# Token groups split on chip, 16-bit turns, joint gates and a folded right side in a fused transformer layer

## What is computed

```python
h = einsum('bhid,oi,od->bho', x, weighted_sum, weight)   # x: 4 x 512 x 256 x 4
h = concatenate([h, txt], axis=1)                        # 589 rows a batch
n = layernorm(h)
gate = sigmoid(relu(n @ gate_w1 + b1) @ gate_w2 + b2)    # 64, then 32 wide
S = cumsum(n @ V_w, axis=1)                              # over the rows
y = (gate * (n @ U_w) * S) @ out_w + out_b
h = h + conv3(n, conv_w) + y                             # three taps along the rows
m = layernorm(h)
q, s = round(m / s), max|m| / 127 per row                # the same for rhs, per column
h = h + (q @ q_rhs) * s * s_rhs
```

## Time and profile before

| | |
|---|---|
| Median of three timed runs | 111.67 us (110.92 to 111.87) |
| Profiled execution | 110.85 us, its span 109.0 us |
| TensorE busy | 98.9 us (91%) |
| VectorE busy | 82.7 us (76%) |
| ScalarE busy | 71.2 us (65%) |
| GpSimd busy | 63.7 us (58%) |
| Moved by transfers | 17.30 MB, 159 GB/s on average |

### The profile page before, as it was taken

How to read it: one execution, slowest core, us unless ns; L and a number is a source line. 1 busy time by engine, 2 the same in 40 slices (tenths; PEclk the granted TensorE clock), 3 DMA queues, 4 the chain that set the end, 5 groups by cost and what they waited for, 6 DMA issues and landing times.

```text
span 109.0 us, 2062 instructions
## 1 busy us (share of the span) xinstructions
PE 98.9 (91%) x660; PEld 85.3 (78%) x660; DVE 82.7 (76%) x239; ACT 71.2 (65%) x144; POOL 63.7 (58%) x111
## 2 busy tenths in 40 slices
PE   5999999999999999999999899997999879788630
PEld 5888888868878899799889799776996669676510
DVE  1456359653387678899897979989799799997991
...
GB/s 61 332 332 362 112 325 51 253 314 206 162 177 302 271 182 111 260 245 165 238 232 177 206 96 179 93 48 150 29 0 99 0 96 35 96 3 0 96 125 125
DMA packets 7993, 17.30 MB, mean 159 GB/s; under 512 B 839, under 2 KB 4783, under 8 KB 7855
## 3 DMA queue, kind: packets, MB, share of 16 engines
q0 software_dynamic: 2880, 10.49, 42.8%
...
q10 hardware_dynamic: 432, 0.27, 0.9%
...
## 4 chain that ended last, share of the span: by engine, by line
PE 65%; DVE 14%; ACT 7%; DMA 5%; issue 5%; POOL 2%; DVEq 0%; ACTq 0%
PE h_ps L796 20%; PE h_ps L808 7%; PE h_ps L810 6%; PE h_ps L812 6%; DMA x_low<-x_dram 5%; PE uvg_ps L873 5%; DVE tmp L752 4%; PE uvg_ps L880 4%; PE xt_ps L857 3%; PE acc_ps L938 2%; DVE nstep L726 2%; PE acc_ps L945 2%; ACT glob L541 2%; DVE amax L724 2%; DVE lscale L746 2%
## 5 line engine op out<-in xcount | busy, mean ns | idle before, releaser
L808 PE MATMUL h_ps<-w_high,x_high 128*128 128x256 f32 x80 | 24.2, 303 | 0.5 <-DMA x_low<-x_dram 0.5
L796 PE MATMUL h_ps<-w_tok,x_sb 128*128 128x256 f32 x96 | 22.5, 389 | 0.0
L810 PE MATMUL h_ps<-w_low,x_high 128*128 128x256 f32 x80 | 22.4, 279 | 0.0
L812 PE MATMUL h_ps<-w_high,x_low 128*128 128x256 f32 x80 | 22.3, 279 | 0.0
L796 PEld LDWEIGHTS h_ps<-w_tok,x_sb 128*128 128x128 f32 x96 | 18.4, 196 | 3.0 <-issue 0.4
L808 PEld LDWEIGHTS h_ps<-w_high,x_high 128*128 128x128 f32 x80 | 15.0, 188 | 3.0 <-issue 2.1
L369 POOL TENSOR_SCALAR rstd<-mv 128x2 f32<-128x2 f32 (+2 forms) x21 | 6.8, 322 | 17.0 <-DVE mv L623 16.6
L370 POOL TENSOR_TENSOR rstd<-rstd,exponent 128x2 f32<-128x2 f32 (+2 forms) x21 | 14.9, 712 | 1.7
L620 DVE BATCH_NORM_STATS2 stats<-h_ps 128x6 f32<-128x256 f32 (+1 forms) x36 | 13.6, 416 | 3.0 <-PE h_ps L796 2.8
L810 PEld LDWEIGHTS h_ps<-w_low,x_high 128*128 128x128 f32 x80 | 15.1, 188 | 0.1
L812 PEld LDWEIGHTS h_ps<-w_high,x_low 128*128 128x128 f32 x80 | 15.0, 188 | 0.0
...
## 6 DMA issues: line engine op xcount, KB each, us to landing
...
```

What stands on the lines that cost most here:

```text
L796: last = nc.tensor.matmul(h_of(g)[:, t, :], x_sb[:, g % 2, kc, t * P:(t + 1) * P], w_tok[:, kc, :], start=(kc == 0 and t == 0), stop=(kc = ...
L808: nc.tensor.matmul(h_of(g)[:, t, :], x_high[:, g % RING, kc, at], w_high[:, kc, :], start=(kc == 0 and t == 0), stop=False, skip_group_che ...
L810: nc.tensor.matmul(h_of(g)[:, t, :], x_high[:, g % RING, kc, at], w_low[:, kc, :], start=False, stop=False, skip_group_check=True)
L812: last = nc.tensor.matmul(h_of(g)[:, t, :], x_low[:, g % RING, kc, at], w_high[:, kc, :], start=False, stop=(kc == KC - 1), skip_group_che ...
```

## The change

It has these parts.
- *Split on chip.* Only group 0 stays plain (`PLAIN` = 1). For groups 1 to 3 (`BY_DMA` = 4) x comes by SyncE's plain loads into three slots; ScalarE rounds it (`chip_high`), and VectorE (groups 1 and 2, `chip_low`) or GpSimd (group 3, `pool_low`) subtracts, in two halves each. Group 3 needs none of the rounding and adding transfers any more.
- *16-bit turns.* The rounded values get another constant, so that the lower 16 bits of each hold the whole number, and `q_turn` transposes those 16 bits alone.
- *Gates.* Both halves' hidden rows lie in one tile of 128 rows, w2 stands twice on a diagonal of 128 x 128, and one product, one sigmoid and one GpSimd product of 64 rows serve a batch. Gate rows now land in the bank of the turns.
- *Text rows* are copied into the bank by ScalarE (`put_txt`).
- *Folded right side.* From item 8 (`FIN_ON_DVE`) qrhs times the column scales is split once into high and low; the product uses both, with whole numbers in 32 bits, and VectorE writes `fin` from the bank in one operation.
- Shift and row scale are made by GpSimd; the right side's column scales are spread by turns in place of products; h2 and the folded right side lie in x's slots.
- The tables of places are new from end to end.

The diff, cut:

```diff
-    gates=(273, 417, 561, 641, 865, 914, 1015, 1022),
-    sigmoid=(7, 20, 33, 40, 62, 65, 77, 83),
...
+    pool_low0=(-1, -1, -1, 4),
+    pool_low1=(-1, -1, -1, 6),
...
+    gates=(-1, 417, -1, 657, -1, 898, -1, 1023),
+    sigmoid=(-1, 22, -1, 45, -1, 68, -1, 86),
...
+    chip_high0=(-1, 1, 4, 10),
+    chip_high1=(-1, 2, 6, 15),
+    chip_low0=(-1, 1, 5),
+    chip_low1=(-1, 2, 8),
...
-FIN_ON_DVE = 10
-PLAIN = 3
...
+FIN_ON_DVE = 8
+PLAIN = 1
+BY_DMA = 4
 RING = 3
+X_SLOTS = 3
...
+            load_x(sp, 1, 0)
+            load_x(sp, 1, 1)
+            sp.dma_start(par_sb[:, :], par).then_inc(par_loaded, 16)
             sp.dma_start(txt_sb[:, :, :], txt.rearrange("b t d -> t b d")).then_inc(txt_loaded, 16)
-            load_x(sp, 1, 0)
-            sp.dma_start(par_sb[:, :], par).then_inc(par_loaded, 16)
-            load_x(sp, 1, 1)
+            load_x(sp, 2, 0)
+            load_x(sp, 2, 1)
             sp.dma_start(rhs_sb[:, :, :], rhs).then_inc(rhs_loaded, 16)
-            for g in range(2, PLAIN):
-                sp.wait_ge(tok_done, g - 1)
-                load_x(sp, g, 0)
+            sp.wait_ge(tok_done, 1)
+            for n in range(2):
+                load_x(sp, 3, n)
...
+            def pool_low(g, n):
+                pool.wait_ge(chip_high_ready[n], g - PLAIN + 1)
+                nc.gpsimd.tensor_tensor(x_low[:, g % RING, HALF_KC[n], :], x_sb[:, g % X_SLOTS, HALF_KC[n], :],
+                                        x_high[:, g % RING, HALF_KC[n], :].bitcast(F32),
+                                        ALU.subtract).then_inc(chip_low_ready[g - PLAIN][n], 1)
...
+                    pool.wait_ge(rstd1_ready, g + 1)
+                    for n in (2 * g, 2 * g + 1):
+                        last = nc.gpsimd.tensor_scalar(shift1[:, n:n + 1], mv1[:, n, 0:1], rstd1[:, n:n + 1], -1.0,
+                                                       ALU.mult, ALU.mult)
+                    last.then_inc(shift1_ready, 1)
...
+                for j in items(place, "lscale"):
+                    _, _, nt, rows = item(j)
+                    pool.wait_ge(qmul_ready, j + 1)
+                    pool.wait_ge(rstd2_ready, j + 1)
+                    nc.gpsimd.tensor_tensor(lscale[0:rows, j, 0:nt], nstep[0:rows, j, 0:nt], rstd2[0:rows, j, 0:nt],
+                                            ALU.mult).then_inc(lscale_ready, 1)
...
+            def chip_high(g, n):
+                act.wait_ge(x_loaded[g][n], 16)
+                if g - RING >= PLAIN:
+                    act.wait_ge(tok_done, g - RING + 1)
+                nc.scalar.activation(x_high[:, g % RING, HALF_KC[n], :], x_sb[:, g % X_SLOTS, HALF_KC[n], :],
+                                     ACT.Copy).then_inc(chip_high_ready[n], 1)
+
+            def rhs_fold_high():
+                act.wait_ge(srhs_ready, 1)
+                nc.scalar.activation(srhs_high[:, :, :], srhs[:, :, :], ACT.Copy).then_inc(srhs_rounded, 1)
...
+            def put_txt(b):
+
+                j = ITEMS_PER_B * b + HALVES
+                act.wait_ge(h2_ready, j if b < B - 2 else j - 1 if b < B - 1 else LAST - 1)
+                nc.scalar.activation(h_item(j)[0:T, 0, :], txt_sb[:, b, :], ACT.Copy).then_inc(txt_put, 1)
...
+                    nc.scalar.activation(gate[:, b % 2, :], xt_ps[0:HALVES * R, 0:PAIR], ACT.Sigmoid,
                                          bias=b2).then_inc(gate_ready, 1)
...
+                    dst = qT if j < FIN_ON_DVE else qT_wide
+                    nc.scalar.activation(dst[:, j % 2, :, 0:nt * rows], q16_v[:, :, 0:nt * rows].bitcast(I16),
+                                         ACT.Copy, bias=-LOW_ZERO).then_inc(qT_ready, 1)
...
+            def chip_low(g, n):
+                dve.wait_ge(chip_high_ready[n], g - PLAIN + 1)
+                nc.vector.tensor_tensor(x_low[:, g % RING, HALF_KC[n], :], x_sb[:, g % X_SLOTS, HALF_KC[n], :],
+                                        x_high[:, g % RING, HALF_KC[n], :].bitcast(F32),
+                                        ALU.subtract).then_inc(chip_low_ready[g - PLAIN][n], 1)
...
+            def rhs_fold():
+                dve.wait_ge(rhs_ready, 1)
+                for c in range(CB):
+                    last = nc.vector.tensor_tensor(srhs[:, c, :], qrhs[:, c, :], rs_row[:, :], ALU.mult)
+                last.then_inc(srhs_ready, 1)
+
+            def rhs_fold_low():
+                dve.wait_ge(srhs_rounded, 1)
+                nc.vector.tensor_tensor(srhs_low[:, :, :], srhs[:, :, :], srhs_high[:, :, :].bitcast(F32),
+                                        ALU.subtract).then_inc(srhs_split, 1)
...
-                for g in groups(place, "shift"):
-                    dve.wait_ge(rstd1_ready, g + 1)
-                    nc.vector.scalar_tensor_tensor(out=shift1[:, 2 * g:2 * g + 2],
-                                                   in0=mv1[:, 2 * g:2 * g + 2, 0], scalar=-1.0,
-                                                   in1=rstd1[:, 2 * g:2 * g + 2], op0=ALU.mult,
-                                                   op1=ALU.mult).then_inc(shift1_ready, 1)
...
-                    dve.wait_ge(rstd2_ready, j + 1)
-                    then_wait(nc.vector.tensor_tensor(lscale[0:rows, j, 0:nt], nstep[0:rows, j, 0:nt],
-                                                      rstd2[0:rows, j, 0:nt], ALU.mult))
+                    dve.wait_ge(lscale_ready, j + 1)
                     dve.wait_ge(acc_done, j + 1)
+                    if j >= FIN_ON_DVE:
+                        dve.wait_ge(h2_ready, j + 1)
+                        dve.wait_ge(out_stored[j % 4], 16 * (j // 4))
+                        for t in range(nt):
+                            last = nc.vector.scalar_tensor_tensor(out=fin[0:rows, j % 4, t, :],
+                                                                  in0=acc_v[0:rows, t, :],
+                                                                  scalar=lscale[0:rows, j, t:t + 1],
+                                                                  in1=h2[0:rows, j % 4, t, :], op0=ALU.mult,
+                                                                  op1=ALU.add)
+                        last.then_inc(fin_dve, 1)
+                        continue
...
+                    if kc % (KC // 2) == 0 and g < BY_DMA:
+                        pe.wait_ge(chip_high_ready[half_kc], g - PLAIN + 1)
+                        pe.wait_ge(chip_low_ready[g - PLAIN][half_kc], 1)
...
-                pe.wait_ge(hid_ready, g + 1)
-                nc.tensor.matmul(uvg_ps[0:R, 0:PAIR], w2, hid[:, g % 2, :], start=True,
+                b = g // HALVES
+                pe.wait_ge(hid_ready, HALVES * (b + 1))
+                nc.tensor.matmul(xt_ps[:, 0:PAIR], w2, hid[:, b % 2, :], start=True,
                                  stop=True).then_inc(gate_done, 1)
...
-                    nc.tensor.matmul(h_item(j)[0:rows, 0, :], ident[0:T, 0:T], txt_sb[:, b, :], start=True,
-                                     stop=False, skip_group_check=True)
+                    pe.wait_ge(txt_put, b + 1)
...
+                        last = nc.tensor.transpose(q16_v[:, c, t * P:t * P + rows],
+                                                   v_low[0:rows, j % 2, t, c * P:(c + 1) * P, 0],
+                                                   ident16[0:rows, 0:rows])
...
+                        if j < FIN_ON_DVE:
+                            last = nc.tensor.matmul(acc_v[0:rows, t, :], qT[:, j % 2, c, at], qrhs[:, c, :],
+                                                    start=(t == 0 and c == 0), stop=(c == CB - 1), skip_group_check=True)
+                        else:
+                            pe.wait_ge(srhs_split, 1)
+                            for n, part in enumerate((srhs_high, srhs_low)):
+                                last = nc.tensor.matmul(acc_v[0:rows, t, :], qT_wide[:, j % 2, c, at], part[:, c, :],
+                                                        start=(t == 0 and c == 0 and n == 0),
+                                                        stop=(c == CB - 1 and n == 1), skip_group_check=True)
```

279 lines of the change are left out of this document (160 added, 119 removed).

## The result

The changed kernel takes **107.54 us** (median of six runs, 107.19 to 108.13) against 111.02 (110.33 to 111.87) for the kernel before, a ratio of 0.9686 (95% interval 0.9631 to 0.9741). It is 3.5 us faster. The forecast was 102.5 us with a range of 99.2 to 106.5: the direction was right, the size was not, and the time lies outside the range.

A forecast was written before the change was run, and what follows sets the result against it. TensorE was taken to bound the kernel up to 41.2 us, VectorE's queue after. Span 109.0 - 3.1 - 5.7 = 100.2 us, 102.05 with time outside, plus 0.45 for the median: 102.5 us, range 99.2 to 106.5.

The forecast's parts named there:

- The head: Up to the end of group 3's products, 41.2 us before: TensorE-bound, forecast -3.1 us, bounds 0 and -4.4.
- The 16-bit turns: TensorE's turns of 16-bit blocks take half as long or just as long: saving 0 to 2.2 us, 1.0 taken.
- The late part: From 41.2 us to the end, VectorE's queue leads: forecast -5.7 us, bounds -5.2 and -7.8.
- Net -5.2 us: VectorE's late queue: scale products, additions, shifts and a copy go out, the fold's 1.5 us comes in.
- over 90%: Sign of being right late: VectorE busy over 90% from the end of group 3's products to the last addition.
- the 3.4 us: VectorE's twelve scale products leaving its late queue: 8 x 0.345 + 4 x 0.147 us.
- is no work at all: Part of the scale products' price: one 128 x 2 step took 1.58 us at 102.51, where others take 0.16.
- most of it would be hidden: Head: GpSimd's two subtractions may hold VectorE up to 4.8 us, where it has 10 us to spare, less 4.9.
- the second one has no cause left: Tail: VectorE's 1.58 us step at 102.51 would go, since GpSimd no longer adds items 8 and 9.
- GpSimd becomes the queue: Rival: after 41.2 us GpSimd's in-order queue has hardly any slack, +2.4 to +4 us; chance 0.23 for 104.5 to 107.5.
- The clock falls: Rival: holes around 70 us drop TensorE's grant to 1.2 GHz, products behind take twice their time, 114.5 us; chance 0.03.
- The split halves come late: Rival: in the head, group 1's data or ScalarE's roundings slip, TensorE stands, 3.1 us lost, 105.6 us; chance 0.07.

The follow-up runs named there:

- e5: Kernel before, with GpSimd's ten additions (items 0 to 9) replaced by constant fills that read no SBUF: 108.32 us, ratio 0.9792.
- e3: Changed kernel with twelve warming products of 128 columns where TensorE idles ahead of the mix of item 3: 106.77 us, ratio 0.9573.
- e13: Changed kernel with the additions of items 0 and 1 made by VectorE, the other six left on GpSimd: 103.57 us, ratio 0.9310.
- e6: Changed kernel with the twelve small row scales on VectorE again, right ahead of each product's step: 107.41 us, ratio 0.9683.
- e4: Changed kernel with each of GpSimd's eight additions (items 0 to 7) replaced by two constant fills that read no SBUF: 101.85 us, ratio 0.9139.
- e11: Changed kernel with each of GpSimd's eight additions replaced by one operation that reads one SBUF tile: 101.80 us, ratio 0.9164.
- e2: Changed kernel with the issue of group 6's two adding transfers moved behind GpSimd's addition of item 0: 105.76 us, ratio 0.9470.

## Why the prediction was wrong

**The head: right within 0.4 us.** Forecast -3.1 with bounds 0 and -4.4, measured -2.7. Group 1's halves were there in time: group 0's last product, two records, starts at 12.04 and the first rounded one at 12.38 with no idle time. GpSimd's two subtractions took 2.50 us each on average (forecast 2.4). They held VectorE (a 128 x 2 step of 0.17 us at 24.98 took 1.72, a pair of taps at 30.04 took 1.46 for 1.03), and all of it was hidden, as that rival allowed.

**The 16-bit turns: mis-sized, the upper bound holds.** I took 1.0 us between 0 and 2.2. The chain of the changed kernel has four of them in half the time of the 32-bit ones:

```profile
78.78 0.44 PE xt_ps L973 x4
...
79.66 0.22 PE qt_ps L1041 x4
```

**The late part: the step that failed.** Its sum was "Net -5.2 us" on VectorE and "Late part: -5.7 us". Measured: VectorE -1.3 us (58.75 to 57.46), the time 0.0 in the profiled executions. VectorE was busy 85% of the late part, where "over 90%" was the sign of being right. Three things were wrong in the sum.

1. *Prices that held standing time.* The durations were means of groups. The 0.345 us of a scale product held a step of 1.58; in e5 the mean is 0.166, so the eight were priced 1.4 us too high. The 0.227 of a shift held a step of 0.69 in the head; the five late ones take 0.16, another 0.3. I even noted that a part of the 3.4 us "is no work at all", and expected the cause to go with items 8 and 9. With the additions' reads away in both kernels VectorE's late work falls by 54.60 - 51.63 = 3.0 us, not 5.2. The standing was not removed with the steps on which it fell: in the new order it fell on other steps (`nstep` and the low halves above all), and grew from 4.1 to 5.8 us. -3.0 + 1.7 is the -1.3 measured.
2. *A price for standing that depends on its place.* 4.1 us of it cost 2.0 us of time before, so about half of it fell where the kernel had slack; which steps those were is not traced. After, half of it falls on the low half for which TensorE's queue waits (2.74 us), with the clock's share on top (0.8 us of the end by e3). The mechanism was in the prediction, in the paragraph on the head alone, "most of it would be hidden"; for the late part I wrote that "the second one has no cause left" and never laid the eight additions that stay beside VectorE's new order, step by step. e13 shows that two of them made 4 us.
3. *The rest of the late estimate was 1.5 us too high.* Without the reads the late part gives 65.8 - 61.6 = 4.2 us, not 5.7: 3.0 us of VectorE's work and 1.2 us of its idle time (11.2 to 10.0), where the sum had 5.2 and 0.5. So the overpricing of the first point more than accounts for it.

**The rivals.** *GpSimd becomes the queue* had the measured time at the edge of its range (104.5 to 107.5), but not for its reason: VectorE waits for no shift or scale of GpSimd's, ScalarE 2.3 us in all, below the 3 us that the prediction set as its mark, and giving the scales back to VectorE changed nothing (e6); that the number is close is luck. What its last sentences said of an addition that holds VectorE was the true cause, put in the wrong stretch. *The clock falls* happened in small, 0.55 of full speed over 57.4 to 61.2 us, at a stall and not from thin work. *The split halves come late* didn't happen.

The Trainium skill (SBUF — State Buffer, Who interferes with whom) has a two-input VectorE instruction exclude a GpSimd instruction that reads SBUF. The rows agree for GpSimd's additions: the low half took 3.28 us beside one, and 0.44 with fills in their place (e4). It also says that the issue order decides which of the two waits. The pair of rows in e11 agrees: whichever step started second was the long one. The low half at 53.64 does not, by its record: it starts before the addition's row begins and was held all the same.

**What stays open.** Why an addition that stands right behind two transfer issues holds VectorE for about 3 us (3.28 in the changed kernel, 4.23 for the taps in e6) and one without them for 1.5 (e2); whether the rows of GpSimd start too late, or the engine keeps VectorE out while it still issues, no run told apart. What a one-input read of GpSimd's of an addition's length would cost is open too. 0.4 us of the first point were not traced to single steps.
